# Three sets of f32 transposes per turn move from TensorE to 16-bit transfers, in the last stage of an eight-block attention and feed-forward kernel

## The reference, cut to what matters

```python
x = x + tanh(g_xattn[1]) * xattn1(layernorm(x), ctx, ...)     # stage "c"
x = x + tanh(g_ffn[1])   * ffn1(layernorm(x), ...)            # stage "d"

# xattn1, for the 256 image keys that the context has:
q = rms_norm(x @ q_w.T + q_b) * norm_q_w          # 16 heads of 32
k = rms_norm(ctx @ k_img_w.T + k_img_b) * norm_k_img_w
v = ctx @ v_img_w.T + v_img_b
out = softmax(q @ k.T / sqrt(32)) @ v             # per head
return out @ o_w.T + o_b
# ffn1: rms norm, 8-bit activations, ternary weights
u = value * silu(gate);  return bitlinear(u, w_out)
```

## Time and profile before

| | us |
|---|---|
| median of 3 runs (lowest, highest) | 1090.17 (1089.71, 1090.85) |
| the profiled execution | 1090.44 |
| its span, first to last instruction | 1088.7 |
| turn 3 / turns 4, 5, 6 / turn 7 | 58.21 / 56.73, 56.74, 56.73 / 56.11 |
| from turn 7 to the end | 101.35 |

### The profile page before, as it was taken

How to read it: one execution, slowest core, us unless ns; L and a number is a source line. 1 busy time by engine, 2 the same in 40 slices (tenths; PEclk the granted TensorE clock), 3 DMA queues, 4 the chain that set the end, 5 groups by cost and what they waited for, 6 DMA issues and landing times.

```text
span 1088.7 us, 24800 instructions
## 1 busy us (share of the span) xinstructions
PE 1066.6 (98%) x10042; PEld 639.5 (59%) x10042; DVE 832.1 (76%) x1439; ACT 530.2 (49%) x871; POOL 117.1 (11%) x212
## 2 busy tenths in 40 slices
PE   9799999999999999999999999999999999999998
PEld 3455555555777777777777655545454545454544
DVE  4888888778777666575676577898887878787987
ACT  4676777676433333333333344445363636363633
POOL 1101001010000000000000221230202011110110
PEclk9999999999999999999999999999999999999999
DMA  9565654552232130230220021104031312111133
GB/s 363 198 207 174 194 179 138 181 156 66 112 79 51 37 79 20 59 90 18 69 59 20 20 88 40 49 2 96 12 67 42 60 48 41 49 31 39 32 67 78
DMA packets 83616, 92.83 MB, mean 85 GB/s; under 512 B 57264, under 2 KB 57776, under 8 KB 83248
## 3 DMA queue, kind: packets, MB, share of 16 engines
q1 hardware_dynamic: 83504, 91.25, 28.7%
HBM read 65.02 MB, written 12.58 MB: 71 GB/s over the span
## 4 chain that ended last, share of the span: by engine, by line
PE 90%; DVE 5%; issue 2%; ACT 1%; DMA 1%; SPq 0%; POOL 0%; DVEq 0%; ACTq 0%; POOLq 0%
PE bank L755 10%; PE bank L649 10%; PE bank L650 10%; PE bank L737 10%; PE bank L614 10%; PE bank L860 8%; PE bank L848 5%; PE bank L878 4%; PE bank L494 4%; PE bank L829 3%; PE bank L810 3%; PE bank L579 2%; PE bank L519 2%; PE bank L546 2%; PE bank L567 2%
## 5 line engine op out<-in xcount | busy, mean ns | idle before, releaser
L649 PE MATMUL bank<-ARENA,W 128*128 128x256 f16 x1024 | 227.3, 273 | 0.7 <-issue 0.7
L650 PE MATMUL bank<-ARENA,W 128*128 128x256 f16 x1024 | 227.3, 273 | 0.0
L737 PE MATMUL bank<-W,ARENA 128*128 128x512 bf16 x512 | 120.8, 379 | 0.0
L860 PE MATMUL bank<-W,ARENA 128*128 128x512 bf16 x512 | 117.8, 379 | 1.1 <-DVE W L1780 0.5
L614 PE MATMUL bank<-ARENA 128*128 128x512 f32 x256 | 118.1, 604 | 0.3 <-DMA ARENA<-in_wkv 0.3
L755 PE MATMUL bank<-ARENA 128*128 128x512 f32 x256 | 116.8, 600 | 0.5 <-DVE ARENA L1708 0.5
L1050 ACT ACTIVATE ARENA<-ARENA 128x512 f16<-128x512 f32 x78 | 48.3, 627 | 132.8 <-DVE ARENA L1630 132.8
L649 PEld LDWEIGHTS bank<-ARENA,W 128*128 128x128 bf16 x1024 | 100.2, 98 | 19.2 <-issue 1.3
L650 PEld LDWEIGHTS bank<-ARENA,W 128*128 128x128 bf16 x1024 | 100.2, 98 | 18.0
L1251 ACT ACTIVATE ARENA<-bank,ARENA 128x512 f32<-128x512 f32 x64 | 43.5, 685 | 119.6 <-PE bank L860 113.5
L2077 POOL TENSOR_TENSOR ARENA<-ARENA 128x2 f32<-128x2 f32 (+1 forms) x72 | 49.6, 689 | 468.7 <-DVE ARENA L1406 235.1
(11 more groups left out here) (185 smaller groups left out, 1741.8 us busy)
## 6 DMA issues: line engine op xcount, KB each, us to landing
W<-in_w SPq DMA_DIRECT2D x48, 512.0 KB, 4.3
ARENA<-in_w SPq DMA_DIRECT2D x24, 512.0 KB, 3.6
kv_store<-ARENA SPq DMA_DIRECT2D x32, 256.0 KB, 4.2
W<-kv_store SPq DMA_DIRECT2D x15, 512.0 KB, 4.4
ARENA<-in_ctxT SPq DMA_DIRECT2D x8, 512.0 KB, 3.9
X<-in_x SPq DMA_DIRECT2D x8, 512.0 KB, 5.8
ARENA<-in_ctx SPq DMA_DIRECT2D x8, 512.0 KB, 6.0
out<-X SPq DMA_DIRECT2D x15, 256.0 KB, 2.3
```

Of the source, the lines that this page charges most:

```text
L649: pe.matmul(bank[:, i * S:(i + 1) * S], W0[:, at:at + P], xt_half(b, 0)[:, k, :], start=(k == 0), stop=False)
L650: mm = pe.matmul(bank[:, i * S:(i + 1) * S], W0[:, at:at + P], xt_half(b, 1)[:, k, :], start=False, stop=(k == KD - 1))
L737: mm = pe.matmul(banks[6 + t], hx(q, what)[:, i * S + t * P:i * S + (t + 1) * P], W0[:, UP_AT + m * D:UP_AT + (m + 1) * D], start=(m == 0 ...
L860: mm = pe.matmul(to, QQ[d][:, t, k * P:(k + 1) * P], W1[:, at:at + D], start=(k == 0), stop=(k == KD - 1))
```

## The change

In turns 3 to 7 TensorE turns no keys and queries, and no tokens for blocks 4 to 7. Instead ScalarE parts the f32 values, read as pairs of 16-bit integers, into a plane of low halves and one of high halves (`c_part_k`, `c_part_q`, `c_part_x`: two copies of 128x1024 elements each); one transfer turns both planes (`turn_keys`, `turn_queries`, `turn_tokens`: 512 KB each, all into one place, `planes`); and ScalarE joins them into f32 again (`c_join_k`, `c_join_q`, `c_join_x`: two such copies each, written with a step of two elements). Keys are parted into `F`, queries from `F` into `xn`, tokens from `xn` into `F`, with waits for the transfer that read the place before. The product of the norm weights is made once as a row `wqk` (a transfer and one VectorE product), and `c_norm_q` multiplies by it. Keys and values get one place where they had two, and are loaded a block later. The orders of the five engines change, as the diff shows; in TensorE's the last four matmuls of `d_out_product(d, 0)` come behind weigh 2.

```diff
@@ SyncE @@
 def load_keys_of(f): ...
-                sp.wait_ge(s.c_kt, max(0, 2 * (f - 1)))
+                if f > 3:
+                    sp.wait_ge(s.c_ks, 2 * (f - 3))
+                else:
+                    sp.wait_ge(s.c_kt, 2 * f if f > 1 else 0)
 def load_values_of(f):
-                sp.wait_ge(s.c_pv, max(0, 4 * (f - 1)))
+                sp.wait_ge(s.c_pv, 4 * f)
+            def turn_planes(src, done):
+                sp.dma_start_transpose(bufW["planes"].rearrange("p a b -> p (a b)").rearrange("p (n s) -> p n s", s=P),
+                                       bufC[src + "16"].rearrange("p a b -> p (a b)")).then_inc(done, 16)
+            def turn_keys(f):
+                sp.wait_ge(s.c_ks, 2 * (f - 2))
+                sp.wait_ge(s.c_xtr, 2 * f + 2)
+                sp.wait_ge(s.c_kd, 16 * (f - 3))
+                turn_planes("F", s.c_kd)
+            def turn_queries(f):
+                sp.wait_ge(s.c_qs, 2 * (f - 2))
+                sp.wait_ge(s.c_ktr, 2 * f + 2)
+                sp.wait_ge(s.c_qd, 16 * (f - 3))
+                turn_planes("xn", s.c_qd)
+            def turn_tokens(f):
+                sp.wait_ge(s.c_xs, 2 * (f - 3))
+                sp.wait_ge(s.c_qtr, 4 * f)
+                sp.wait_ge(s.c_xd, 16 * (f - 4))
+                turn_planes("F", s.c_xd)
...
+            for turn in range(3, NB):
+                f, c, d = turn, turn - 2, turn - 3
                 if d > 0:
                     store_out(d - 1, 1)
+                turn_keys(f)
+                if f + 1 < NB:
+                    load_keys_of(f + 1)
+                turn_u(d, 0)
+                turn_q(c)
+                turn_u(d, 1)
+                turn_queries(f)
+                store_out(d, 0)
+                if f + 1 < NB:
+                    turn_tokens(f + 1)
+                load_values_of(f)
@@ TensorE @@
 def c_project_q(f, t):
-                pe.wait_ge(s.c_xtr, 2 * f + t + 1)
+                pe.wait_ge(s.c_xtr, 2 * f + (t + 1 if f < 4 else TB))
 for turn in range(3, NB): ...
                 c_scores(b, 2)
                 if turn == 3:
                     c_turn_x(3)
-                c_turn_k(f)
                 c_project_q(f, 0)
...
                 c_probs(b, 2)
-                c_turn_q(f)
                 c_weigh(b, 1)
-                d_out_product(d, 0)
+                d_out_product(d, 0, 0, KH - KH // 4)
                 c_probs(b, 3)
                 c_weigh(b, 2)
-                if f + 1 < NB:
-                    c_turn_x(f + 1)
+                d_out_product(d, 0, KH - KH // 4)
                 c_weigh(b, 3)
                 d_out_product(d, 1)
@@ ScalarE @@
+            def c_part_q(f, t):
+                act.wait_ge(s.c_qn, 2 * f + t + 1)
+                if f == 3:
+                    act.wait_ge(s.c_xt, 2 * f + 2)
+                copy(parted(bufC["xn16"], t), halves(bufC["F16"][:, t, :])).then_inc(s.c_qs, 1)
+            def c_join(to, done, each):
+                for k in range(2):
+                    copy(to[:, 2 * k:2 * k + 2, :].rearrange("p c (s h) -> p h c s", h=2),
+                         bufW["planes"].rearrange("p (h c) s -> p h c s", h=2)[:, :, 2 * k:2 * k + 2, :]).then_inc(done, each)
+            def c_join_q(f):
+                act.wait_ge(s.c_st, max(0, 16 * (f - 1)))
+                act.wait_ge(s.c_qd, 16 * (f - 2))
+                c_join(bufW["QT16"][:, f % 2 * KD:(f % 2 + 1) * KD, :], s.c_qtr, 2)
 for turn in range(3, NB): ...
                 d_gate(d, 1)
+                if turn > 3:
+                    c_join_x(f)
                 c_square_k(f, 0)
...
-                c_turn_k(f)
+                c_part_k(f, 0)
+                c_part_k(f, 1)
                 c_square_q(f, 0)
...
                 c_probs(b, 0)
+                c_join_k(f)
                 c_square_q(f, 1)
                 c_probs(b, 1)
+                both(d_round_u, d, 1)
                 c_probs(b, 2)
-                both(d_round_u, d, 1)
-                c_turn_q(f)
+                c_part_q(f, 0)
+                c_part_q(f, 1)
                 c_probs(b, 3)
+                c_join_q(f)
                 if f + 1 < NB:
-                    c_turn_x(f + 1)
+                    c_part_x(f + 1, 0)
+                    c_part_x(f + 1, 1)
                 warm(ACT.Silu)
@@ VectorE @@
 def c_norm_q(f, t):
+                v.wait_ge(s.c_qinv, 2 * f + t + 1)
+                if f > 2:
+                    v.wait_ge(s.c_kd, 16 * (f - 2))
+                    v.wait_ge(s.c_row, 1)
+                    v.scalar_tensor_tensor(out=bufC["F"][:, t, :], in0=bank_c(f"pq{t}", f)[0], scalar=keep["sm"][:, 2, t:t + 1], in1=bufW["wqk"],
+                                           op0=ALU.mult, op1=ALU.mult).then_inc(s.c_qn, 1)
+                    return
 def c_norm_x(f):
-                v.wait_ge(s.c_xt, 2 * f)
+                if f > 3:
+                    v.wait_ge(s.c_qd, 16 * (f - 3))
+                else:
+                    v.wait_ge(s.c_xt, 2 * f)
...
             c_weigh(0, 3)
+            v.wait_ge(s.ld_nq, 16)
+            v.tensor_tensor(bufW["wqk"], bufC["h"][:, 0, :], bufC["h"][:, 1, :], ALU.mult).then_inc(s.c_row, 1)
 for turn in range(3, NB): ...
                 c_norm_q(f, 1)
                 c_weigh(b, 0)
+                d_integers16(d, 1)
+                c_weigh(b, 1)
                 if f + 1 < NB:
                     stats(f + 1, s.c_ve)
-                c_weigh(b, 1)
-                d_integers16(d, 1)
-                d_store(d, 0)
+                c_weigh(b, 2)
                 if f + 1 < NB:
                     c_norm_x(f + 1)
-                c_weigh(b, 2)
+                d_store(d, 0)
                 c_weigh(b, 3)
                 d_store(d, 1)
```

More of the change, by code:

```diff
@@ L45 @@
     c_ve c_rstd c_xn c_xt c_xtr c_kss c_kinv c_kn c_kt c_ktr c_sc c_scr c_mhl c_mt c_mtr c_st c_ex
+    c_ks c_kd c_qs c_qd c_xs c_xd c_row ld_nq
     c_pv c_pvr c_pjq c_qss c_qinv c_qn c_qt c_qtr c_po c_xo c_const c_vb c_vo c_vor c_bias c_xb
@@ L150, in strip, with build @@
     return corners(bank)[:, :, m * DH:(m + 1) * DH]
-def build(nc, x, ctx, ctxT, gates, w0, w1, wkv, wqo, vec, wnorm, cols, cst, masks, selq, selc, out):
+def build(nc, x, ctx, ctxT, gates, w0, w1, wkv, wqo, vec, wnorm, wqk, cols, cst, masks, selq, selc, out):
     with ExitStack() as stack:
@@ L190, in build @@
         w0f = W0[:, :].bitcast(F32)
-        bufW = area(w0f, [("K", (2 * TB, D), F32), ("KT", (2 * KD, S), F32), ("QT", (2 * KD, S), F32), ("V", (2 * TB, D), F32),
-                          ("u", (TB, HID), F32)])
+        bufW = area(w0f, [("K", (TB, D), F32), ("KT", (2 * KD, S), F32), ("QT", (2 * KD, S), F32), ("V", (TB, D), F32),
+                          ("u", (TB, HID), F32), ("planes", (2 * KD, S), U16T), ("wqk", (D,), F32)])
+        bufW.update({n + "16": v for n, v in area(w0f, [("K", (TB, 2 * D), U16T), ("KT", (2 * KD, 2 * S), U16T), ("QT", (2 * KD, 2 * S), U16T)]).items()})
         vbs = bufB["left"].rearrange("p (k c) -> p k c", k=KD)
@@ L198, in build @@
                                                                           ("MHL", (TB, P), BF16)]))
+        bufC.update({n + "16": v for n, v in area(below, [("wqo", (2, KD * D), F32), ("F", (TB, 2 * D), U16T), ("xn", (TB, 2 * D), U16T)]).items()})
+        CT16 = CT.rearrange("p k s -> p (k s)").bitcast(U16T).rearrange("p (k s) -> p k s", k=KD)
         diag = scrA["raw0"][:, 0, 0:P]
@@ L262, in build @@
         for turn in range(3, NB):
-            places.turn(turn, ("g0 v1 g3 pq0 v6 w0 y0 xt1", "v0 po1 v3 g4 v5 g7 tq1 w2", "po0 g2 kt0 v4 v7 pq1 w1 w3",
-                               "g1 v2 kt1 g5 g6 mt tq0 xt0 y1"))
+            places.turn(turn, ("g0 v1 g3 pq0 v6 w0 y0", "v0 po1 v3 g4 v5 g7 w2", "po0 g2 v4 v7 pq1 w1 w3", "g1 v2 g5 g6 mt y1"))
         places.turn(NB, ("g0 v1 g3 v5 v7 w1 w3", "v0 v3 g6 g7 y0", "po0 g2 g4 g5 mt w0", "g1 v2 v4 v6 po1 w2"))
@@ L302, in build, with halves, parted @@
         QQ[NB - 1] = bufC["PT"][:, 4, :].bitcast(BF16).rearrange("p (t d) -> p t d", t=TB)
+        def halves(v):
+            return v.rearrange("p (c s h) -> p h c s", s=P, h=2)
+        def parted(v, t):
+            return v.rearrange("p a b -> p (a b)").rearrange("p (h c t s) -> p t h c s", h=2, c=KD, t=TB)[:, t, :, :, :]
         def half(n):
@@ L457, in sync_program @@
             sp.dma_start(bufC["wn"], wnorm).then_inc(s.ld_wn, 16)
[L458 to L461, removed]
+            sp.wait_ge(s.b_w1, 3 * NB)
+            sp.wait_ge(s.b_pr, 8 * NB)
+            sp.dma_start(bufC["h"].rearrange("p t d -> p (t d)"), wqk).then_inc(s.ld_nq, 16)
+            for turn in range(1, 3):
+                load_keys_of(turn + 1)
+                if turn == 2:
+                    turn_q(0)
+                load_values_of(turn)
+            for turn in range(3, NB):
+                f, c, d = turn, turn - 2, turn - 3
                 if d > 0:
                     store_out(d - 1, 1)
[L464 to L472, removed]
+                turn_keys(f)
```

(4 more changed lines are left out.)

26 lines of the change are left out of this document (22 added, 4 removed).

## The result

The changed kernel takes 1105.36 us (median of 4 runs, 1104.87 to 1106.51), beside 1089.99 us for the kernel before (4 runs): ratio 1.0141, with a 95% interval of 1.0124 to 1.0159. It is slower, by 15.4 us; the forecast was 1101.4, with a range from 1094 to 1112. The profiled execution took 1105.8 us for a span of 1103.9, so it can be set against the 1088.7 of before line by line.

A forecast was written before the change was run, and what follows sets the result against it. TensorE, busy 98% of the span, was taken as the bound; turns 4 to 6 (+6.3), turn 3 (+1.9), turn 7 (+2.7) and the weight row (+0.35) sum to +11.2 us, giving 1101.4 us, range 1094 to 1112.

The forecast's parts named there:

- What leaves TensorE: TensorE, removed transposes of keys, queries and tokens: 13.8 us at most, of which only queries and tokens can shorten a turn.
- The keys' group: TensorE at scores 3: removing 0.93 us of transposes gives nothing, as it then waits about 1.1 us for VectorE's reduction.
- The queue of SyncE: Split product 0 delays `turn_u(d, 1)` and the queries queued behind it: a turn becomes 58.8 us instead of 56.73, +2.1.
- theory A: The prediction's own account: product 0, `turn_u(d, 1)`, the queries' transfer behind it, `c_join_q` and next scores set the turn's length.
- The choice of 56.5 over 55.5: Queries' landing, us into the turn: 56.5 if their data stands behind the first transfer's, 55.5 if nothing holds it.
- The joining: ScalarE's `c_join_q` at the turn's end: a pair of 16-bit copies takes 2.1 us, next scores start at 58.8.
- The landing of the queries: The queries' transfer, issued behind `turn_u(d, 1)` from 51.2 at the earliest, lands 56.5 us into the turn.
- Turn 3 and turn 7: Turn 3 grows 1.9 us, gaining 0.2 from its keys; turn 7 grows 2.7, having had no tokens to turn before.
- The row `wqk`: One-time VectorE product of the two weight rows, 0.7 us, ahead of the scores of batch 1: charged 0.35 us.
- The covers: Keys' transfer hidden with 1.5 us to spare; token joining delays `c_norm_k` to 12.9, still covered by 0.1 us before `v2`.
- The clock: Sign of a wrong forecast, without a size: a granted clock under 1.00 behind the new idle time.
- The rival of the other sign: Transfers stay hidden in each turn, so only removed work counts: -9.2 us, 1081; chance 0.11.

The follow-up runs named there:

- experiment 4: The changed kernel with the keys turned by TensorE again, queries and tokens as in the change: 1105.69 us, ratio 1.0141 to the kernel before.
- experiment 1: The changed kernel with SyncE sending `turn_queries(f)` ahead of `turn_u(d, 1)`: 1099.28 us, ratio 1.0080 to the kernel before.
- experiment 2: The changed kernel with `d_out_product(d, 0)` in one piece ahead of `c_probs(b, 3)`, as before the change: 1089.5 us, ratio 0.9994 to the kernel before.
- experiment 3: The changed kernel with a second place for `u` in block 0 of `X` in turns 4 to 7, product 0 still split: 1087.21 us, ratio 0.9971.
- experiment 5: The changed kernel with twelve needless matmuls ahead of product 1 in turns 3 to 7: 1105.55 us, ratio 1.0133 to the kernel before.
- experiment 6: The kernel of experiment 1 with eleven needless matmuls ahead of product 1 in turns 3 to 7: 1097.88 us, ratio 1.0062 to the kernel before.
- experiment 7: The kernel of experiment 3 with VectorE's reduction of scores 2 moved ahead of `d_weighted(c)`: 1085.68 us, ratio 0.9953 to the kernel before.
- experiment 8: The kernel of experiment 7 with product 0 of turn 3 in one piece: 1083.9 us, ratio 0.9930 to the kernel before.

## Why the prediction was right

The sign, the place and the mechanism came out as written; the size was 4.0 us short of 15.2 (span against span, 11.2 forecast).

**What leaves TensorE.** The keys' group gives nothing: the wait of 0.95 us at scores 3 stands where 0.93 was removed, the forecast said about 1.1, and experiment 4 puts the keys back at no cost in the total. The row behind it, an end and a start 0.12 apart in the earlier trace rows, was enough to see it.

**The queue of SyncE.** Product 0 was to end 49.26 into the turn and ends at 49.55 (813.20) in turn 4 and 49.37 in turn 5. In turn 4 the issue follows 0.17 behind, and product 1 starts 4.77 behind the end; over the five turns it is 4.73 to 5.23 (forecast 4.56), and the wait is 2.8 to 3.3 (2.7). Queries were to land at 56.5; ScalarE starts to join them at 56.72, 57.25, 56.64 and 57.05 in turns 4 to 7. Experiment 1 isolates the queries' place, experiments 2 and 3 the wait for `d_y`, and each took its part away where theory A said. The choice of 56.5 over 55.5, on the ground that the engines are full for a single transfer, was right: the two lie end to end.

**The terms mis-sized.** Set against 58.8 (60.1 for turn 3) the five turns are 0.37, 0.75, 1.04, 0.84 and 0.84 us too long, 3.8 of the missing 4.0. Three terms make this up.
- The joining. The forecast held the price per element on ScalarE to be one, whatever the types, and put the pair at 2.1 us, as for the parting. The parting takes 2.0, the joining 2.53 to 2.55. As the forecast had 0.2 us more between landing and scores, of which hardly any was used, scores start 2.59 behind the start of the joining and not 2.3. That is 0.29 a turn, 1.5 in all.
- The landing of the queries, 0.1 to 0.8 us behind 56.5, 1.7 in all. Most of it is in turns 5 and 7, where the issue of `turn_u(d, 1)` took 3.15 and 2.97 us and not the 1.7 of the forecast, so that the queries' issue began 52.8 and 52.6 into the turn and not 51.7, as it did in turns 4 and 6.
- Product 1 at the lower clock in turns 4 and 6, 0.65 in all, a term that the forecast didn't have.

The last 0.23 us are in the last stretch, which was to stay as it is. They arise 31 us into it, where fourteen of the products of `c_probs` (L873) take 1.50 us and not 1.23; why stays open.

**Turn 3 and turn 7.** +2.27 and +3.53, beside 1.9 and 2.7 forecast, both short by the same terms. The row `wqk` and what else lies ahead of turn 3: 0.34 for 0.35, which is luck. The same work ahead of turn 3 ends between 702.70 and 704.16 us in the executions of experiments 1 to 3 and 5 to 8, so one execution of each kernel can't show a term of this size.

**The covers.** Keys' transfer hidden in turns 4 to 7, `c_norm_k` in time though tokens are joined in 2.54 and not 2.1: both held. The joining begins at 8.0 and its squares at 10.4 into turn 4, so `c_norm_k` starts at 13.0, where 12.9 was forecast, and ends at 14.5, still ahead of `v2`.

**The clock** was named as what would make the forecast wrong, with no size. It did fall in turns 4 and 6, and cost only 0.24 and 0.41 us there, where the product was 1.69 longer. That was luck of the order: the queries' chain was nearly as long as the slower product. In experiment 1, where no wait follows product 1, the same fall cost the full 1.7 and 1.4 us.

**The rival of the other sign** (transfers hidden, 1081) fell for this kernel, but its mechanism is real. With a second place for `u` the product doesn't wait, and a turn takes 54.8 to 55.1 in experiment 3, beside that rival's 54.7. The 54.3 to 54.7 of experiments 7 and 8 also have VectorE's other order. What took the wait away was another place for one buffer; a faster transfer wasn't tried.

## What to carry to other kernels

Before a piece of work is split or moved later, look which semaphore its last instruction raises and what is queued behind the wait for it: here four matmuls, 0.9 us together, held back two transfers that both ended on the critical path, and cost 16 us in five turns (1.0141 beside 0.9994 in experiment 2). Where a transfer waits for the reader of a single place, look for a second place, such as a tensor that is dead by then: here it took the wait away in four turns (experiment 3). And of several groups taken off a busy engine, only those count whose next instruction doesn't already wait for another engine; find that by comparing an end with the next start before counting the gain.

## What was not expected of the hardware

**TensorE's clock after a short idle time.** Product 1 of turn 4 in stretches (granted clock third from the end), behind 2.84 us without work:

```profile
815.13:817.97 2.84, 0.00 (x0) 0.03 (x1) 0.00 (x0) 0.00 (x0) 0.00 (x0) 1.00 1.12 209
...
818.50:819.50 1.00, 1.00 (x4) 0.33 (x3) 0.00 (x0) 0.00 (x0) 0.00 (x0) 0.50 1.12 211
819.50:820.50 1.00, 1.00 (x4) 0.43 (x3) 0.21 (x1) 0.13 (x1) 0.00 (x0) 0.50 0.14 30
820.50:821.10 0.60, 0.60 (x3) 0.15 (x1) 0.60 (x2) 0.60 (x1) 0.00 (x0) 0.50 0.00 0
821.10:821.60 0.50, 0.50 (x3) 0.15 (x2) 0.50 (x2) 0.50 (x2) 0.00 (x0) 0.52 0.00 0
821.60:822.10 0.50, 0.50 (x4) 0.26 (x3) 0.50 (x2) 0.50 (x2) 0.00 (x0) 1.00 0.00 0
```

From about 818.2 to 821.6 the clock is at its lower level, 1.2 GHz, then back at 2.4. It doesn't follow from the length of the idle time alone: in the changed kernel it fell behind 2.84 and 2.83 us (turns 4 and 6), and stayed at 2.4 GHz behind 2.80, 3.29 and 2.94 (turns 3, 5, 7). In experiment 1 it fell behind 2.65 and 2.66, and stayed behind 3.08, 2.65 and 3.07. In experiment 4 it fell behind 3.41, 2.86 and 2.85, and stayed behind 2.87 and 2.77; in turn 3 of experiments 3 and 7 it stayed behind 2.85 and 2.84. It also fell behind less: in turn 3 of experiment 8 after waits of 1.47 and 0.39 us with 0.27 us of work between them. What decides stays open. Idle time of TensorE goes before each of these falls, and with the time before product 1 filled, in experiments 5 and 6, product 1 took 3.6 us in all ten turns.

**ScalarE's 16-bit copies.** Two of 128x1024 elements take 2.02 us when the output is contiguous and the input has the step of two (the parting), and 2.55 when the output has it (the joining), beside 1.94 for two of f32 from PSUM. So the joining pair is 0.5 us dearer than the parting pair. No run has such a copy without a step, so what the step on the input costs isn't shown.

**The issue of a 512 KB transpose** takes SyncE 1.3 to 3.2 us in the changed kernel, mostly 1.8 to 2.1, and isn't steady from turn to turn. Where `turn_u(d, 1)` took 1.80 to 1.85, the queries' issue behind it took 2.48 to 2.59; where it took 3.15 or 2.97, the queries' took 1.93 and 1.98. The turns 5 and 7 of experiment 5, with the short issue first, are 0.9 and 0.7 us shorter than those of the changed kernel with the long one. What makes an issue long isn't known.
